# A graph layer's lead-in: one-hots written in pieces of the lanes, and frame 0 added ahead of frame 1's one-hots

## What is computed

```
def _ngcf_conv(x, W1, W2, src, dst, n_nodes):
    deg_out = clip(segment_sum(ones, src), 1.0)
    deg_in = clip(segment_sum(ones, dst), 1.0)
    norm = rsqrt(deg_out[src] * deg_in[dst])
    msg = (x[src] @ W1 + x[src] * x[dst] @ W2) * norm[:, None]
    agg = segment_sum(msg, dst)
    return x @ W1 + agg
h = _ngcf_conv(x, W1_1, W2_1, src, dst, n); h = relu(h)
h = _ngcf_conv(h, W1_2, W2_2, src, dst, n)
return layernorm(x + h)
```

## Time and profile before

| what | value |
|---|---|
| median of 3 runs | 1142.33 us (1139.75 to 1142.66) |
| profiled execution, its own time | 1141.05 us |
| its span in the profile | 1139.3 us |
| busy: PE, DVE, ACT, POOL | 821.3, 990.9, 736.3, 833.9 us |
| gathers: early, layer 0, layer 1 | 48, 346, 394 |

### The profile page before, as it was taken

How to read it: one execution, slowest core, us unless ns; L and a number is a source line. 1 busy time by engine, 2 the same in 40 slices (tenths; PEclk the granted TensorE clock), 3 DMA queues, 4 the chain that set the end, 5 groups by cost and what they waited for, 6 DMA issues and landing times. The chain is left out here.

```text
span 1139.3 us, 33680 instructions
## 1 busy us (share of the span) xinstructions
PE 821.3 (72%) x13104; PEld 754.9 (66%) x13104; DVE 990.9 (87%) x2382; ACT 736.3 (65%) x2733; POOL 833.9 (73%) x811
## 2 busy tenths in 40 slices
PE   1676567888888877777773677777777877778774
PEld 0565356787787867677773676676667776667764
DVE  8999888999999977777775479989998999899997
ACT  2200235888888987777772367667766787677775
POOL 7388777777777777777764777777777777777771
PEclk9999877988989998878887779989998889898997
DMA  9976312322222322222233233444444334443333
GB/s 208 191 226 260 114 27 51 82 69 66 80 66 67 81 67 67 54 67 68 68 67 91 51 76 83 97 94 103 92 90 92 86 89 89 94 93 86 88 82 66
DMA packets 148545, 105.05 MB, mean 92 GB/s; under 512 B 115752, under 2 KB 128744, under 8 KB 147820
## 3 DMA queue, kind: packets, MB, share of 16 engines
q1 hardware_dynamic: 123032, 71.17, 22.8%
q0 software_dynamic: 25216, 32.50, 15.7%
q10 hardware_dynamic: 212, 0.42, 0.1%
HBM read 58.92 MB, written 45.11 MB: 91 GB/s over the span
## 5 line engine op out<-in xcount | busy, mean ns | idle before, releaser
L819 POOL DMA_INDIRECT c_rows<-table,k_row_i x394 | 383.7, 974 | 136.6 <-issue 119.8
L819 POOL DMA_INDIRECT k_rows<-table,k_row_i x346 | 348.3, 1007 | 105.5 <-issue 105.2
L878 PE MATMUL c_out<-k_wcat,c_uvt 128*128 128x64 f32 x1516 | 216.6, 304 | 71.2 <-ACT c_uvt L960 68.9
L878 PEld LDWEIGHTS c_out<-k_wcat,c_uvt 128*128 128x128 f32 x1516 | 210.7, 220 | 86.1 <-ACT c_uvt L960 55.7
L951 ACT ACTIVATE c_sum<-c_sum,k_xh 128x64 f32<-128x64 f32 x762 | 164.4, 307 | 156.4 <-DVE c_sum L1170 155.9
L1111 DVE TENSOR_SCALAR c_sel<-k_place,k_grid 128x512 bf16<-128x512 f16 (+1 forms) x788 | 245.3, 379 | 0.0
L852 PE MATMUL c_sum<-c_rows,c_sel 128*128 128x64 bf16 x4701 | 169.8, 202 | 46.6 <-DVE c_rows L1121 45.9
L852 PEld LDWEIGHTS c_sum<-c_rows,c_sel 128*128 128x128 bf16 x4701 | 166.5, 104 | 50.5 <-issue 48.9
L938 ACT ACTIVATE c_own<-k_xh 128x64 f32<-128x64 f32 x762 | 195.2, 387 | 0.0
L852 PE MATMUL c_sum<-c_yr,c_sel 128*128 128x64 bf16 x1567 | 179.0, 206 | 1.8 <-DVE c_lo L1141 1.8
L852 PE MATMUL c_sum<-c_rest,c_sel 128*128 128x64 bf16 x1567 | 178.0, 207 | 0.0
(11 more groups left out here) (209 smaller groups left out, 1230.8 us busy)
## 6 DMA issues: line engine op xcount, KB each, us to landing
table<-c_y SPq DMA_DIRECT2D x47, 384.0 KB
out<-c_y SPq DMA_DIRECT2D x47, 256.0 KB, 2.6
c_res<-in_x SPq DMA_DIRECT2D x46, 256.0 KB
c_rows<-table,k_row_i POOLq DMA_INDIRECT x394
k_rows<-table,k_row_i POOLq DMA_INDIRECT x346
table<-k_xh SPq DMA_DIRECT2D x1, 3640.0 KB
table<-k_xh SPq DMA_DIRECT2D x2, 1820.0 KB
table<-k_xh SPq DMA_DIRECT2D x1, 3575.0 KB
```

Of the source, the lines that this page charges most:

```text
L819: nc.gpsimd.indirect_dma_start(out=rows[:, b % RING, i], out_offset=None, in_=tables[l], in_offset=bass.IndirectOffsetOnAxis(ap=k.row_i[:, ...
L878: last = nc.tensor.matmul(out_bank(g)[:, n, :], uvt[:, g % 2, n, :], weights, start=True, stop=True)
```

## The change

The order on the vector engine at the start of the lead-in is another: `hots(1)` stands behind `spreads(0)` and no longer ahead of the relative tiles, and the first one-hot of frame 1 (`hots(2)`) stands behind `add(0)` and `early_rows`. And from piece 3 on, a one-hot is made in several instructions, each for a part of the 128 lanes: three parts for the pieces of frames 0 to 5, two for 32-column pieces, one for the last. The semaphore is released by the last part.

```
@@ -58,6 +58,8 @@
 SPAN = 64
 PIECES = [(k, b, 4) for k in range(7) for b in (0, 4)] + [(7, 0, 8), (8, 0, 8)]
+LANE_CUTS = {4 * FRAME_PS[0]: (0, 43, 86, P), 32: (0, 64, P), 8 * FRAME_PS[-1]: (0, P)}
+WHOLE_PIECES = 3
 LAST_PIECE = [max(i for i, p in enumerate(PIECES) if p[0] == k) for k in range(FRAMES)]
@@ -446,9 +448,13 @@
                 if i >= 3:
                     dve.wait_ge(piece_placed, i - 2)
                 w = FRAME_PS[f]
-                shape = [P, P, nb, w]
-                V.tensor_tensor(hot[i % 3][:, :, 0:nb * w].rearrange("q l (b p) -> q l b p", b=nb), lanes[:, :, 0:w].unsqueeze(2).to_broadcast(shape),
-                                by_raw(lane_t, f, b0, nb).unsqueeze(1).to_broadcast(shape), ALU.is_equal).then_inc(hots_made, 1)
+                cuts = LANE_CUTS[nb * w] if i >= WHOLE_PIECES else (0, P)
+                for l0, l1 in zip(cuts, cuts[1:]):
+                    shape = [P, l1 - l0, nb, w]
+                    last = V.tensor_tensor(hot[i % 3][:, l0:l1, 0:nb * w].rearrange("q l (b p) -> q l b p", b=nb),
+                                           lanes[:, l0:l1, 0:w].unsqueeze(2).to_broadcast(shape),
+                                           by_raw(lane_t, f, b0, nb).unsqueeze(1).to_broadcast(shape), ALU.is_equal)
+                last.then_inc(hots_made, 1)
@@ -532,8 +538,6 @@
             hots(0)
-            dve.wait_ge(halves_made, 2)
-            hots(1)
             dve.wait_ge(halves_made, 5)
@@ -541,13 +545,16 @@
             spreads(0)
+            hots(1)
             for f in range(1, 6):
                 spreads(f)
-                hots(2 * f)
+                if f - 1 not in EARLY_FRAMES:
+                    hots(2 * f)
                 add(f - 1)
                 if f - 1 in EARLY_FRAMES:
                     a, b = EARLY_FRAMES[f - 1]
                     early_rows(8 * a, 8 * b)
+                    hots(2 * f)
                 hots(2 * f + 1)
```

## The result

The changed kernel takes 1133.25 us (median of 5 runs, 1130.84 to 1135.10), the kernel before 1142.33 (5 runs, 1139.75 to 1144.81). The ratio is 0.9925, with a 95% interval of 0.9902 to 0.9948. The prediction was 1133.0, with a range of 1129.3 to 1138.5.

What follows compares the result with a forecast made beforehand. GpSimd, issuing all gathers, was taken as the bound. The ring's 14.0 us slack less 2.7 vector delay, 0.9 wake and 1.0 later loss gave 9.4: profiled 1141.05 to 1131.7, median 1133.0 us, range 1129.3 to 1138.5.

Steps and rivals of the forecast that it cites:

- The bound: Whole kernel: its time is the sum of GpSimd's own stretches, since GpSimd issues all gathers and hardly waits.
- the start: Lead-in: the new order brings row numbers and first gather 2.5 us earlier, at 44.7; vector engine's lead-in 1.3 later.
- the thirds: One-hots from piece 3: 21 more instructions at 0.07 us, 1.4 us more vector time; one gather passes per third.
- the ring: Layer 0, batch 13: it waits for batch 5's scaling; 14.0 us slack, less 2.7 and 0.9, leaves 10.4.
- the early gathers: Lead-in: 48 gathers at 1.3 us each after the first, ending about 110 instead of 141, 31 us earlier.
- what is kept until the end: Layer 0 after batch 13: gathers beside a busier vector engine lose 1.0 us of the gain, at most 3.5.
- A: One-hots: seams let no waiting gather in; gain only 0.5 to 2.5 us, about 1141; chance 0.10.
- B: One-hots: a gather let in holds the next third 0.81 us; 1156 us; chance 0.04 including other losses.
- no early gather over 2.2 us: Lead-in sign: apart from the first, every early gather stays within 2.2 us, the 48 averaging near 1.1.
- the step that failed: Layer 0: gathers slow from 100/78 to 100/75 us only beside extra vector work, at most 8 batches, 3.5 us.
- Sum: Whole kernel: 14.0 - 2.7 - 0.9 - 1.0 = 9.4 us gained.
- this layer moves as a block: Layer 1: with the turn between layers it shifts earlier as a whole, its first gather near 602.2.

Runs made afterwards that it cites:

- The ring of nine: Changed kernel with a ring of 9 batches instead of 8 in layer 0; 1747.58 us, ratio 1.0156, and 1737.70 us, ratio 1.0181.
- e2: Kernel before with only the one-hots cut in thirds, in the old order; 1750.93 us, ratio 1.0161.
- the kernel with one tile: Changed kernel with GpSimd writing one small constant tile behind each gather; 1720.78 us, ratio 1.0003.
- the kernel with two tiles: Changed kernel with GpSimd writing two small constant tiles behind each gather; 1422.79 us, ratio 0.8270.
- h1: Changed kernel with GpSimd writing three small constant tiles behind each of the 48 early gathers only; 1670.72 us, ratio 0.9941.

## Why the prediction was right

The bound, the start, the thirds and the ring were foreseen as they came. Two terms were mis-sized, the early gathers and what is kept until the end, and that the total agrees to 0.2 us is luck.

**Start.** Every term held to 0.1 us: the relative tiles at 31.41 (31.4), the new stall for ScalarE's copies 0.79 (0.7), `add(0)` at 42.61 after 1.38 (42.65 after 1.35), the first gather at 44.70 (44.7). The runs with one part alone give it to the order: 44.7 with it, 47.3 without, on their chips too.

**Thirds.** 0.07 a cut was right, and a gather let in at a seam costs the vector engine nothing (rivals A and B are out: 4.02 for three thirds with gathers in between; B wanted 2 us for each). The vector engine's first scaling in layer 0 starts at 133.4 where the earlier trace rows have 130.7: 2.7 later, as summed.

```profile
L1140 DVE TENSOR_TENSOR c_yr<-k_rows x51: 281/678/764, 133.4 to 594.1; 128x512 f32<-128x512 f32 x48, 128x256 f32<-128x256 f32 x2, 128x128 f32<-128x128 f32 x1
```

The Trainium skill (SBUF — State Buffer, Who interferes with whom) says of a vector instruction in a two-port mode and GpSimd that whoever issues first has the shared pair for its whole instruction; rival B left that scope out. If it held for these one-hots too, a gather of 0.95 let in ahead of a third would hold the third; the 4.02 show that it doesn't.

**Early gathers.** This term was mis-sized. I took 1.3 for each and an end near 110; they end at 118.80 + 0.94 = 119.74, (119.74 - 44.70) / 48 = 1.56 each. The sum counted a wait of at most one third, 1.32, and left out that the gather's own 0.8 comes after it; so it lasts up to 2.1, as the rows at 48.87 and 53.87 show. Seven of the 48 last over 1.9 us. One of them, at 112.08, takes 2.66, beside the last one-hot, which isn't cut; the sign "no early gather over 2.2 us" missed there. All this cost nothing, as it only took from the wait for the table: 6.4 instead of some 14. The first table gather is at 126.13 (125).

**The ring.** It decides as predicted, and at the batch predicted: the wait is before batch 13 (4.20), with none after. Batch 12, where I had expected 2 to 4 us too, has 0.42, of which 0.30 is the fixed gap. Batch 13 starts at 200.95 (202.4 was forecast), since the wake after the scaling is 200.95 - (199.99 + 0.69) = 0.27 and not 0.9, and the vector engine's lag had shrunk from 2.7 to 199.99 - 198.09 = 1.9. In the sum: 14.0 - 1.9 - 0.3 = 11.8, and 212.81 - 200.95 = 11.9 measured, where I had 10.4.

**What is kept.** Here the prediction was wrong in size, by more than its bound. Of the 11.9, only 593.84 - 587.95 = 5.9 are left at the end of layer 0; I had taken 1.0 of loss and 3.5 as the most (64 gathers at 100/75 instead of 100/78 us are 3.3), and it is 6.0. Matching gathers show where: the first gather of batch 30 comes at 397.04 before and at 385.71 after, 11.3 earlier, so only 0.5 is lost until there; batch 36 comes at 459.32 and 449.26, 10.1 earlier. These are the windows between these gathers and from batch 36 to the end of layer 0 (columns as in the earlier trace rows), before:

```profile
397.04:459.32 62.28, 45.41 (x782) 42.31 (x777) 47.27 (x111) 49.20 (x188) 47.65 (x48) 0.92 0.26 64
459.32:594.80 135.48, 102.44 (x1647) 97.93 (x1648) 101.38 (x236) 99.88 (x377) 103.45 (x106) 0.85 0.27 64
```

and after:

```profile
385.71:449.26 63.55, 53.54 (x966) 50.26 (x962) 56.83 (x134) 56.37 (x216) 48.92 (x49) 0.92 0.27 69
449.26:588.90 139.64, 103.72 (x1648) 98.78 (x1648) 102.42 (x236) 100.72 (x380) 107.62 (x106) 0.84 0.26 62
```

In the first pair the vector engine does 9.6 us more beside the same gathers, the catching up that I had named, and 1.3 is lost: that size is near my 1.0. In the second pair it does the same work (101.4 and 102.4 us in 236 instructions), and 4.2 is lost all the same: GpSimd is busy 107.6 us for 103.5 with the same 106 gathers, and 22 of them take over 1.02 us where 10 did. So the step that failed is the one by which gathers lose only beside extra vector work, with 3.5 as the most. Gathers also came to fall differently on the same vector instructions. Whether that is chance of one execution or comes back in each stays open. (The vector engine's first wait for a gather, in the middle of the layer, comes at 430.35 and came at 408.36 before; I had forecast 450 for a wait near 400.)

**Sum.** +1.5 at the ring and -5.0 in what is kept leave 5.9 at the turn. Layer 1 gives 1.8 more: the spans differ by 1139.3 - 1131.6 = 7.7. That this layer moves as a block was nearly right. The 1.8 stand in no wait but in the gathers themselves: the 394 of layer 1 take 381.9 us where they took 383.7. The profiled executions differ by 1141.05 - 1134.62 = 6.4 only, since the one of after has 3.0 us around its span and the one of before 1.75. The medians differ by 9.1 us, because the profiled execution of before lay 1.3 under its median and that of after 1.4 above its own. The forecast of 9.3 is thus right to 0.2 in the median by luck: in the span it was 9.4 against 7.7, at the turn 9.4 against 5.9, and layer 1 and the scatter between executions made up for it.

**What stays open.** That the ring and not the early start limits the gain rests on the rows of one execution. The ring of nine was to show it, and ran where the ring was not the question. The share of order and thirds in the 9.1 us was not measured for the same reason.

## What to carry to other kernels

Where GpSimd issues indirect gathers beside two-input vector instructions, read the gathers' durations against the vector engine's timeline: each instruction lets one pass, so cutting a long one into equal parts gives gathers for 0.07 us a cut. Then look at once for the next bound behind them (here a table and a ring with 14 us of slack), and don't count on keeping what is gained at a ring: here 6.0 of 11.9 us were lost again by the end of the layer, 4.2 of them beside unchanged vector work. And a gain that comes from a higher rate of gathers should be timed on more than one chip: this one turned from 0.9925 to 1.017.

## What was not expected of the hardware

On the chips of the experiments TensorE nearly stops, with "issue" as its wait, while indirect gathers follow each other at 1.25 us (at 1.30 on the fifth chip, where no closer spacing was profiled); on the chip of the first runs it does not (1 against 54 matmuls in the same 10 us). A low clock is not the reason: the granted clock is 1.00 in the windows above. At 1.30 us nothing is better (1720.78 us, ratio 1.0003), at 1.53 us the whole kernel is 17 to 19% faster than the kernel before on the same chip. In the stretches of the lead-in in which TensorE stands, no packet of the instruction queues lands (none in 70 to 117 us of e2 and of the kernel with one tile, 4 in the kernel with two tiles on the same chip, 4 in h1, 4 in the changed kernel's first run). It looks like a supply of instructions that gathers at this rate cut off, but only the gathers' spacing was varied; what the queue of instructions does was only observed.
